# The third cross attention: row sums of the last head on TensorE, output products beside them, and maxima folded in two parts

## The reference

```
x = x + xattn(layernorm(x), ctx)
q = (x @ Wq).reshape(B, N, 16, 64)            # N = 128 tokens
k = (context @ Wk).reshape(B, M, 16, 64)      # M = 12544 rows
v = (context @ Wv).reshape(B, M, 16, 64)
sim = einsum('bihd,bjhd->bhij', q, k) * 64 ** -0.5
attn = softmax(sim, axis=-1)
out = einsum('bhij,bjhd->bihd', attn, v).reshape(B, N, 1024)
return out @ Wo
```

## Time and profile before

| | us |
|---|---|
| median of 3 runs (lowest, highest) | 3100.88 (3096.41, 3102.68) |
| the profiled execution | 3094.2 |
| its span, first to last instruction | 3092.5 |
| TensorE busy in the span | 2829.8 |
| VectorE busy | 1791.2 |
| ScalarE busy | 1518.3 |
| GpSimd busy | 753.5 |
| first instruction of the stage, last addition's start | 1559.1, 2436.4 |

### The profile page before, as it was taken

How to read it: one execution, slowest core, us unless ns; L and a number is a source line. 1 busy time by engine, 2 the same in 40 slices (tenths; PEclk the granted TensorE clock), 3 DMA queues, 4 the chain that set the end, 5 groups by cost and what they waited for, 6 DMA issues and landing times. The chain is left out here.

```text
span 3092.5 us, 67322 instructions
## 1 busy us (share of the span) xinstructions
PE 2829.8 (92%) x24071; PEld 1859.4 (60%) x24071; DVE 1791.2 (58%) x3568; ACT 1518.3 (49%) x2408; POOL 753.5 (24%) x402
## 2 busy tenths in 40 slices
PE   8999999998968899999899999999998688999988
PEld 5555555555656566666456565656565584666678
DVE  3223333232343777776648888888888517888532
ACT  2333333333221688778246666666665233656521
POOL 2332231321000000000006666666666300000000
PEclk9999999999988899999899999999998697999979
DMA  7888778787706999996622222222222284565455
GB/s 220 281 275 256 250 256 253 257 250 246 246 25 258 385 359 375 355 359 231 219 95 67 64 65 63 64 64 67 61 67 67 81 253 109 148 155 147 108 203 185
DMA packets 329016, 578.89 MB, mean 187 GB/s; under 512 B 78641, under 2 KB 264833, under 8 KB 321665
## 3 DMA queue, kind: packets, MB, share of 16 engines
q1 hardware_dynamic: 328857, 576.59, 56.5%
HBM read 395.49 MB, written 181.05 MB: 186 GB/s over the span
## 5 line engine op out<-in xcount | busy, mean ns | idle before, releaser
L1668 POOL TENSOR_TENSOR l2x_sums<-l2x_sums,all_S 128x768 f32<-128x768 f32 (+1 forms) x208 | 508.4, 2444 | 192.7 <-ACT all_S L1945 185.5
L1850 DVE TENSOR_TENSOR all_S<-all_S,l2x_minus 128x1024 f32<-128x1024 f32 x224 | 399.7, 1788 | 2.6 <-ACT l2x_minus L1941 2.6
L1710 PE MATMUL l2x_key_bank<-ahead_ctx,early_nat_out 128*64 128x512 f32 (+1 forms) x1536 | 321.9, 540 | 0.0
L1034 DVE CUSTOM_DVE_ANT_0 all_S<-l1x_scores,l1x_bias 128x448 f32<-128x448 f32 x448 | 261.7, 621 | 79.5 <-PE l1x_scores L946 70.6
L648 PE MATMUL prep_work<-prep_wv,prep_ctxT 128*128 128x512 f32 x688 | 300.3, 594 | 0.0
L1831 DVE TENSOR_TENSOR l2x_tops<-l2x_scores,l2x_tops 128x768 f32<-128x768 f32 (+1 forms) x208 | 223.5, 1074 | 117.6 <-PE l2x_scores L1726 117.6
L1270 DVE TENSOR_REDUCE l3x_rowmax<-l3x_scores 128x1 f32<-128x448 f32 x448 | 263.4, 622 | 39.7 <-PE l3x_scores L1190 38.2
L1345 ACT ACTIVATE l3x_pT<-l3x_turned 128x896 f32<-128x896 f32 x224 | 205.0, 917 | 163.8 <-PE l3x_turned L1198 160.6
L1945 ACT ACTIVATE all_S<-all_S 128x1024 f32<-128x1024 f32 x224 | 213.1, 952 | 96.3 <-DVE all_S L1850 96.3
L1101 ACT ACTIVATE all_S<-all_S,l1x_negmax 128x896 f32<-128x896 f32 x224 | 232.8, 1042 | 50.5 <-DVE l1x_negmax L1047 34.6
L1741 PE MATMUL l2x_out<-all_S,l2x_values 128*64 128x128 f32 x3136 | 231.2, 289 | 26.8 <-ACT all_S L1945 13.7
(11 more groups left out here) (661 smaller groups left out, 4507.7 us busy)
## 6 DMA issues: line engine op xcount, KB each, us to landing
l1x_bias<-in_fside_Bx16xSxS_dram SPq DMA_DIRECT2D x112, 896.0 KB, 6.8
scratch_k<-prep_kparts SPq DMA_DIRECT2D x84, 672.0 KB, 3.3
l1x_k_half<-scratch_k SPq DMA_DIRECT2D x32, 1568.0 KB, 9.9
keys_k<-scratch_k SPq DMA_DIRECT2D x32, 1176.0 KB, 7.4
l2x_values<-scratch_v SPq DMA_DIRECT2D x112, 256.0 KB, 2.6
scratch_k<-prep_kparts SPq DMA_DIRECT2D x56, 448.0 KB, 4.8
scratch_v<-prep_st_v SPq DMA_DIRECT2D x11, 2048.0 KB, 9.3
scratch_v<-prep_st_v SPq DMA_DIRECT2D x14, 1536.0 KB, 7.2
```

The source lines that it names most:

```text
L1034: nc.vector.tensor_tensor_reduce(out, s, bias_tile[b // 4][:, b % 4 * HB:(b % 4 + 1) * HB], 1.0, -3.4e38, ALU.add, ALU.max, rowmax[:, b:b ...
L1668: nc.gpsimd.tensor_tensor(sums[odd][:, 0:n], sums[odd][:, 0:n], in_memory(u), ALU.add).then_inc(added, 1)
L1710: last = nc.tensor.matmul(keys_ps[u % 2][half * VW:(half + 1) * VW, 0:n], wk_cur[odd][:, k, :], ahead.piece[u // 2][:, k, c:c + n], start= ...
L1850: nc.vector.tensor_tensor(part, part, minus[:, :].unsqueeze(1).to_broadcast([P, blocks_of(u), P]), ALU.add).then_inc(shifted, 1)
```

## The change

Five edits, all in the third cross attention:

1. The maxima. `take_max` of unit 13 no longer goes through `tops`: it reduces the PSUM scores of its six blocks straight to `top_of_last`. `top_of_blocks` reduces `tops` of the 13 units before it, and is issued after the shift that stands at unit 12. A new `top_of_head` takes the maximum of the two, 128 x 128.
2. The last head's row sums. GpSimd no longer adds for head 15. After the output products of each unit of it, TensorE multiplies each block (as weights) with one column of ones into one PSUM column: 98 matmuls, two records each (`weigh_last`). It counts `added` in GpSimd's place. `sum_last` needs only the join of the halves.
3. The other heads' output. Seven of the eight transposes of `att` go into the tail after unit 6, their copy after the last shift, seven of the eight products with `Wo` after unit 10; only heads 14 and 15 are left for the end. `Wo` is loaded from 4 units of the last head on instead of 10.
4. Order at the end of head 15: TensorE's products of head 14's units 12 and 13 go before and after the transpose of the maximum.
5. TensorE's loop has six heads in its body (2 turns). At the start of the stage, the first two key products go before the norm's transposes, which no longer have the 18 small matmuls ahead.

```diff
-        out_ps = out_bank[:, 0:P]
+        out_ps, last_total_ps = out_bank[:, 0:P], keys_ps[1][:, 0:1]
...
-            nc, ph, com, keys_ps[0][:, 0:D].rearrange("p (k n) -> p k n", k=KT))
+            nc, ph, com, misc[:, 0:D].rearrange("p (k n) -> p k n", k=KT), busy=0)
...
-                sp.wait_ge(weighed, HEADS * UNITS - 4)
+                sp.wait_ge(added, HEADS * UNITS - 10)
+                sp.dma_start(wo, a["L2_xattn_Wo"].rearrange("(k p) n -> p k n", p=P)).then_inc(wo_loaded, 16)
                 sp.wait_ge(added, HEADS * UNITS - 4)
-                sp.dma_start(wo, a["L2_xattn_Wo"].rearrange("(k p) n -> p k n", p=P)).then_inc(wo_loaded, 16)
                 load_next(sp)
...
-                for odd in range(2):
-                    pool_head(HEADS - 2 + odd, odd, more=False)
+                pool_head(HEADS - 2, 0, more=False)
...
+                def weigh_last(u):
+                    weigh(HEADS // 2 - 1, 1, u)
+                    for i in range(blocks_of(u)):
+                        k = first_of(u) + i
+                        last = nc.tensor.matmul(last_total_ps, com.S[:, k * P:(k + 1) * P], ones[:, 0:1],
+                                                start=(k == 0), stop=(k == CH - 1))
+                    last.then_inc(added, 1)
+
+                def sum_last():
+                    pe.wait_ge(parts_ready, HEADS)
+
+                    pe.wait_ge(out_taken, HEADS)
+                    nc.tensor.matmul(sum_ps, out_parts[:, :], select[:, :], start=True, stop=True).then_inc(summed, 1)
...
                     if last:
+                        weigh(pair - 1, 0, UNITS - 2)
                         turn_top(h - 1)
+                        weigh(pair - 1, 0, UNITS - 1)
+                        spread_largest(h - 1)
+                        for u in range(UNITS):
+                            weigh_last(u)
+                            if u == 4:
+                                sum_parts(h - 2)
+                            if u == 6:
+                                for e in range(7):
+                                    turn = nc.tensor.transpose(scores_ps[0][:, e * P:(e + 1) * P],
+                                                               att[:, e * P:(e + 1) * P], com.ident[:, :])
+                                turn.then_inc(attT_in_psum, 1)
+                            if u == 10:
+                                pe.wait_ge(attT_ready, 1)
+                                pe.wait_ge(wo_loaded, 16)
+                                for e in range(7):
+                                    nc.tensor.matmul(keys_ps[0][:, 0:D], attT[:, e, :], wo[:, e, :],
+                                                     start=(e == 0), stop=False)
+                        return
...
+                pe.wait_ge(ctx_loaded[0], 16)
+                key_product(0, 0, 0, first=True)
+                key_product(0, 0, 1, first=True)
                 norm_tensor(pe)
...
-                with pe.Fori(1, HEADS // 2 - 1) as i:
-                    tensor_head(i, 0)
-                    tensor_head(i, 1)
+                with pe.Fori(0, 2) as i:
+                    for n in range(3):
+                        tensor_head(i * 3 + (n + 1), 0)
+                        tensor_head(i * 3 + (n + 1), 1)
...
+                    elif u == UNITS - 1:
+                        nc.vector.tensor_reduce(top_of_last[:, :], by_halves(scores_ps[1][:, :], u)
+                                                .rearrange("p a (b t) -> p t a b", t=P),
+                                                mybir.AxisListType.XY, ALU.max).then_inc(maxed, 1)
...
                 def top_of_blocks(h):
+                    dve.wait_ge(maxed, (h + 1) * UNITS - 1)
+                    nc.vector.reduce_max(top_of_first[:, :], tops[:, :].rearrange("p (b t) -> p t b", t=P),
+                                         AX).then_inc(folded, 1)
+
+                def top_of_head(h):
+                    dve.wait_ge(folded, h + 1)
                     dve.wait_ge(maxed, (h + 1) * UNITS)
-                    nc.vector.reduce_max(top[:, :], tops[:, :].rearrange("p (b t) -> p t b", t=P), AX).then_inc(top_ready, 1)
+                    nc.vector.tensor_tensor(top[:, :], top_of_first[:, :], top_of_last[:, :], ALU.max).then_inc(top_ready, 1)
...
+                            if u == UNITS - 2 and not last:
+                                top_of_blocks(h)
+                        elif u == UNITS - 2:
+                            top_of_blocks(h)
                     if not last:
-                        top_of_blocks(h)
+                        top_of_head(h)
...
-                vector_head(HEADS, 0, last=True)
+                take_largest(HEADS - 1)
+                leave_parts(HEADS - 2)
+                for u in range(UNITS):
+                    shift(HEADS - 1, u)
+                    if u == 3:
+                        sum_of(HEADS - 2, 0)
+                    if u == 8:
+                        divide(HEADS - 2)
+                dve.wait_ge(attT_in_psum, 1)
+                nc.vector.tensor_copy(attT[:, 0:7, :].rearrange("p a b -> p (a b)"),
+                                      scores_ps[0][:, 0:7 * P]).then_inc(attT_ready, 1)
                 leave_parts(HEADS - 1)
-                sum_of(HEADS - 1, 1)
-                divide(HEADS - 1)
...
+                dve.wait_ge(added, HEADS * UNITS)
+                divide(HEADS - 1, last_total_ps)
```

More of the change, by code:

```diff
@@ L1582, in l2_cross_attention @@
         values = [ph.sb(f"values{j}", [P, 8, VW]) for j in range(SLOTS)]
+        top_of_first, top_of_last = (ph.sb(f"top_of_{n}", [P, P]) for n in ("first", "last"))
         tops, top = ph.sb("tops", [P, 1024]), ph.sb("top", [P, P])
@@ L1808, in _ @@
                 tensor_head(HEADS // 2, 0, last=True)
-                for u in range(UNITS - 2, UNITS):
-                    weigh(HEADS // 2 - 1, 1, u)
-                sum_parts(HEADS - 1)
+                sum_last()
                 pe.wait_ge(out_taken, HEADS + 1)
-                for e in range(8):
-                    last = nc.tensor.transpose(scores_ps[0][:, e * P:(e + 1) * P], att[:, e * P:(e + 1) * P], com.ident[:, :])
-                last.then_inc(attT_in_psum, 1)
-                pe.wait_ge(attT_ready, 1)
-                pe.wait_ge(wo_loaded, 16)
-                for e in range(8):
-                    last = nc.tensor.matmul(keys_ps[0][:, 0:D], attT[:, e, :], wo[:, e, :], start=(e == 0), stop=(e == 7))
-                last.then_inc(y_in_psum, 1)
+                nc.tensor.transpose(scores_ps[1][:, 0:P], att[:, 7 * P:8 * P], com.ident[:, :]).then_inc(attT_in_psum, 1)
+                pe.wait_ge(attT_ready, 2)
+                nc.tensor.matmul(keys_ps[0][:, 0:D], attT[:, 7, :], wo[:, 7, :], start=False, stop=True).then_inc(y_in_psum, 1)
             @block.vector
```

30 lines of the change are left out of this document (14 added, 16 removed).

## The result

The changed kernel takes 3114.94 us (median of 6 runs, 3109.95 to 3124.24), the one before 3101.14 (6 runs, 3096.41 to 3102.96). The ratio is 1.0054 (95% interval 1.0041 to 1.0067): 13 to 21 us slower.

| | before | after | difference |
|---|---|---|---|
| before the stage | 1559.14 | 1559.50 | +0.4 |
| start, to the first maximum | 17.74 | 17.77 | 0.0 |
| heads, to head 15's first maximum | 752.90 | 756.05 | +3.2 |
| tail, from there to the stage's end | 107.06 | 125.16 | +18.1 |
| behind the stage | 655.66 | 658.42 | +2.8 |

A forecast was written before the change was run, and what follows sets the result against it. TensorE bounds the body, VectorE and GpSimd the last head, then a serial chain. 9 - 1.1 - 6.4 - 0.7 + 19.5 = +20.3 us on the profiled 3094.2 gives 3114.5; with the runs' median 6.7 higher, 3121.2, range 3102 to 3132.

The forecast's parts named there:

- fold, 13 ends: Heads' ends without a branch: the maximum is ready 0.7 us later, TensorE waits for it in full; +9 us (2 to 13).
- head 0: End of head 0, with no shift: the reduction of 13 units is hidden, TensorE's wait of 1.54 us shrinks by 1.1.
- loop: TensorE's loop of heads: two turns of six heads instead of six of two; -6.4 us, bounds 0 and -10.4.
- start: Stage start: key products go first, query products run wholly at the high clock, first scores come earlier; -0.7 us (-2 to +1).
- tail: Last head to stage end: row sums make TensorE the bound, mostly at the low clock; ends at 2456.3, +19.5 us.
- Wo's load starts after unit 3: Tail: the output weights' load starts after unit 3, is wanted at unit 10, 30 us later, and costs nothing.
- d: Head's end on VectorE: length of the strided reduction of 768 elements from PSUM, taken as 1.5 us; contiguous bound 0.96.
- 4 branches fewer at 1.59 us: TensorE's loop: dropping four branches saves 1.59 us each, 6.4 us together.
- the first (high clock): Rival: the tail runs at the high clock, -7.8 us there instead of +19.5, total 3094 us; chance 0.10.
- The second: Rival: the fold works as meant, maximum 1.07 us earlier at 13 ends, -14 instead of +9, 3098 us; chance 0.06.
- The third: Rival: tail's weight loads cost 0.12 us per record even at the low clock, row sums 23.5 us, 3105 us; chance 0.05.
- The fourth: Rival: the long loop body stalls anyway, once per pair of heads, so the 6.4 us don't come, 3128 us; chance 0.05.

The follow-up runs named there:

- e3: The changed kernel with only the fold of the maxima undone (one reduction over all blocks, as before): 3107.63 us, ratio 1.0033 to before.
- e4: The changed kernel with only TensorE's loop undone (six turns of two heads): 3120.00 us, ratio 1.0071 to before.
- e9: The changed kernel with only the stage's start undone (first two key products again behind the norm's and queries' products): 3114.22 us, ratio 1.0045 to before.
- e1: The changed kernel with the last head's row sums put back from TensorE to GpSimd: 3090.72 us, ratio 0.9973 to before.
- e6: The changed kernel with TensorE's loop removed, its twelve middle heads written out: 3112.04 us, ratio 1.0046 to before.
- e2: The changed kernel with each row sum moving 64 columns of ones instead of one: 3110.66 us, ratio 1.0045 to before.
- e5: The changed kernel with the last head's row sums as products that load 64 columns of ones and move the blocks: 3083.92 us, ratio 0.9955 to before.
- e8: The changed kernel with the edits of e5, e6 and e7 together: 3061.58 us, ratio 0.9887 to before.
- e7: The changed kernel with VectorE's last maxima ahead of its last shift, ScalarE's exponential of that unit behind the next key copy: 3100.12 us, ratio 1.0007 to before.
- f1: e8 with the output weights' load issued earlier, from GpSimd's queue instead of SP's: 3057.53 us, ratio 0.9868 to before.
- f2: e8 without the fold of the maxima: 3078.75 us, ratio 0.9931 to before.

## Why the prediction was right

It said 3121 us, in a range of 3102 to 3132; 3114.94 was measured, and most of the loss was where it was put, in the tail. Its sum was +20.3 us; the ratio of the runs gives +16.7 (13 to 21), the stage in the two traces +21.3, since after's profiled execution lies above its median and before's below. By its terms:

| term | predicted | in the trace | by experiment |
|---|---|---|---|
| fold, 13 ends | +9 | +5.7 (14 at 0.41) | +6.5 with head 0 and dips (e3) |
| head 0 | -1.1 | -1.1 | |
| loop | -6.4 | -2.0 | -1.3 to -5.0, dips counted in (e4) |
| start | -0.7 | 0.0 | 0 (e9) |
| tail | +19.5 | +18.1 | row sums +25.1, the rest -7.0 (e1) |

The loop's -2.0 is 4.15 + 1.55 us above plain heads (heads 7 and 6) against the 7.75 us of the five branches before. Fold, head 0 and loop make +2.6 of the heads' +3.2; the rest is 0.1 to 0.2 us in single heads.

The tail: the mechanism and its size held. Records of row sums were put at 0.205 us and took 0.223 at the low clock, but 68 of the 196 took 0.12 to 0.18, since the clock rose twice, once behind the transposes, where no rise was forecast; together 38.7 us against 40.2. TensorE's stretch from the first product to the last row sum was 66.7 us (2388.03 to 2454.76) against 67.7, and the chain behind it 3.7 against 3.3. The tail's first product came 0.8 us sooner behind the last head's first maximum than before. One step was wrong and cost nothing: "Wo's load starts after unit 3". SP issued it only at 2433.5 us, behind the loads of values in its own queue, 7 us ahead of its use at 2440.6; in the faster tails of e2, e5 and e8 the same place made TensorE wait 2.5 to 6.5 us.

The fold: the sign was right and its cause too, VectorE being behind by the shift: e7 moves the shift (and one exponential of ScalarE with it), and TensorE's wait is gone. The term that was mis-sized is d, the reduction of 768 elements from PSUM: 1.5 was taken from strided reads of SBUF, and 0.944 was measured, the lower bound. The last maximum, 0.39 instead of 0.29, took back a tenth. From the end of the shift to the finished maximum it is 3.32 us (2226.84 to 2230.16) against 2.95.

The loop: the step "4 branches fewer at 1.59 us" failed. The price of a branch is not a constant: it was 1.2 to 4.1 us in the long loop, the gap less the wait that it replaces, and 1.5 to 1.7 more where the clock falls (see e4). A cost that no step had came on top: the clock fell behind a wait of 1.5 us at six ordinary ends in after, e1, e6 and e9, at 1.55 to 1.7 us each. That is 6 of some 90 ends with such a wait; at the 77 where the wait was 1.17 us or less (before, e3, e7, e8, f1, f2) it never fell. In e2, e4 and e5 the wait is 1.5 and no ordinary end dips, so the wait does not suffice; what else decides stays open.

The start: the gain of the query products (8.48 to 7.21) came, and the forecast had left 1.8 us between their end (1565.5 + 0.5 + 7.2 = 1573.2) and the first scores (1575.0), near the wait of 1.92 that came. The 0.7 us went in front of them: the key products were to end 6.0 us behind the stage's start, with a rise of the clock on the way, and ended 6.6 us behind it (1566.06), mostly at the low clock. So the term that was mis-sized is the length of the key products, 5.97 us against 5.5.

The two errors, a fold priced 3.3 us too high and a loop gain put 4.4 too high, cancelled; that the sum came out so near is in part luck. Of the rivals, the first (high clock) was wrong for 36 us and right for 12. The second was wrong, since VectorE was behind at every ordinary end. The third was wrong: the price of a row-sum record goes with the clock, 0.223 against 0.122. The Trainium skill (TensorE: Matmul & The Clock Gate, LDWEIGHTS) gives 107 ns for a load of 128 columns by one formula that names no clock; in this trace a record is near that at the high clock alone. The fourth was wrong: the long loop has one gap, and e6, written out, none. By the same page of the Trainium skill (What's actually happening) activity releases the throttle; here 36 us without a gap did not, nor did 56 us in e6.

## What to carry to other kernels

On TensorE make the small operand the loaded side and the large one the moved side: in this tail the same row sums cost 25 us more than GpSimd's in one form and 6 us less in the other; the form changed both the time of a load and the clock. Before shortening the last link of a chain, look whether its engine is idle ahead of it; if it isn't, move other work from in front first, since fold and late shift each lost alone and gained 0.5 us a head together. When a step is moved forward, look at what its old place had covered, and at which clock it will run in the new one. A price read from one execution (a branch, a start, a tail) can hang on where TensorE's clock happened to fall or rise: here that moved single stretches by 1.5 to 4 us between executions.

## What the runs showed of the hardware

- Unbroken work on TensorE left the clock at 0.50 for 36 us (after) and 56 us (e6) when three fifths of the time went into loading 128 x 128 blocks to move 1 column, and for 35 us with 64 columns (e2). Behind seven transposes among it the clock rose in four of the six traces with 1 column and was soon back at 0.50 (after: 2430 to 2444 us); with 64 columns, one trace, it stayed at 1.00.
- The same row sums with 64 columns of ones loaded and the blocks moved: the clock was at 1.00 some 4 us behind the first product and stayed there for 14 of 14 us (e5, 2388 to 2402).
- 64 moved columns behind such a load cost 0.007 us more per record than 1 (3.68 against 3.57 for 16), at clock 0.50.
- A strided maximum from PSUM took 0.944 us for 768 elements per partition, one from SBUF 1.94 for 1024: 1.23 against 1.90 ns per element.
- A wait of 1.5 us within an otherwise full stretch was followed by a fall of the clock in 6 of some 90 cases, at 1.55 to 1.7 us each, a gap of 2.4 to 3.9 us at the loop's branch in 6 of 17; a wait of 1.17 or less in none of 77.
- TensorE's branch at the end of a loop's body left it idle for 2.4 to 3.9 us; twelve heads written out had no such gap (e6).
